# Third layer's routed experts: tiles of 128 rows in place of 256, result buffers in the room of the residual sums

## The reference

```python
def _L2_ffn_ref(x, router_w, router_bias, sw1, sw3, sw2, ew1, ew2):
    xf = x.reshape(-1, C)                                   # 2048 x 256
    shared_out = jax.nn.silu(xf @ sw1) * (xf @ sw3) @ sw2    # hidden 512
    s = jax.nn.sigmoid(xf @ router_w.T)
    _, topk_idx = jax.lax.top_k(s + router_bias, 2)          # 2 of 8 experts
    s_sel = jnp.take_along_axis(s, topk_idx, axis=1)
    denom = s_sel.sum(axis=1, keepdims=True)
    gates = jnp.where(denom > 1e-09, s_sel / (denom + 1e-09), 1.0 / 2)
    comb = jnp.einsum('nke,nk->ne', jax.nn.one_hot(topk_idx, 8), gates)
    h = jax.nn.gelu(jnp.einsum('nd,edh->neh', xf, ew1))      # hidden 256
    y = jnp.einsum('neh,ehd->ned', h, ew2)
    return shared_out + jnp.einsum('ned,ne->nd', y, comb)
```

## Time and profile before

| What | Value |
|---|---|
| Median of 3 runs | 2845.38 us |
| The profiled execution: its time, its span | 2846.69 us, 2844.9 us |
| PE busy, share of the span | 2314.1 us, 81% |
| DVE, ACT, POOL busy | 1528.4, 934.1, 815.6 us |
| Third layer's shared unit and scatter | up to about 1813 us |
| Tile loop of the third layer | 1813.4 to about 1904.6 us |
| Bytes moved by transfers | 203.25 MB, mean 71 GB/s |

### The profile page before, as it was taken

The page is one execution under the profiler, slowest core; times in us unless marked ns, Lnnn a source line. Parts: engine busy times, 40 slices in busy tenths (PEclk is TensorE's granted clock), DMA queues, the critical chain, the costliest instruction groups (busy, mean ns, idle before and its releaser), DMA issues. The chain is left out here.

```text
span 2844.9 us, 37465 instructions
## 1 busy us (share of the span) xinstructions
PE 2314.1 (81%) x14275; PEld 1526.4 (54%) x14275; DVE 1528.4 (54%) x3005; ACT 934.1 (33%) x1469; POOL 815.6 (29%) x602
## 2 busy tenths in 40 slices
PE   6978849883995982998578876997999997768998
PEld 5755535552884871887245643773434343354554
DVE  3775763465224664000743533235999989835553
ACT  3423313320112341222223320115676674423431
POOL 1120321233002102000240104014797989602221
PEclk9989969996997786999789978998999999979999
DMA  4216010002762103553100002573010110010000
GB/s 149 68 45 227 13 60 1 1 16 101 270 220 82 36 8 142 172 195 131 49 23 1 2 1 93 169 207 111 9 51 26 35 42 19 0 48 1 8 9 15
DMA packets 103793, 203.25 MB, mean 71 GB/s; under 512 B 8832, under 2 KB 79744, under 8 KB 97728
## 3 DMA queue, kind: packets, MB, share of 16 engines
q1 hardware_dynamic: 95936, 179.88, 19.0%
q0 software_dynamic: 7680, 20.98, 2.3%
HBM read 143.02 MB, written 57.80 MB: 71 GB/s over the span
## 5 line engine op out<-in xcount | busy, mean ns | idle before, releaser
L3542 POOL TENSOR_TENSOR l_attn_ring<-l_attn_ring,l_attn_c_rows 128x1024 f32<-128x1024 f32 x128 | 301.6, 2356 | 86.2 <-DVE l_attn_ring L3431 86.2
L3431 DVE TENSOR_TENSOR_SCAN l_attn_ring<-bank,l_attn_ring 128x512 f32<-128x512 f32 x256 | 299.2, 1210 | 23.4 <-ACT bank L3317 18.9
L3161 PE MATMUL bank<-l_attn_ring,identity 128*128 128x512 f32 x512 | 253.3, 618 | 36.0 <-POOL l_attn_ring L3542 29.1
L160 PE MATMUL bank<-x_features,weights 128*128 128x512 f32 x544 | 261.3, 625 | 24.4 <-ACT x_features L3281 8.4
L3317 ACT ACTIVATE bank<-l_attn_step,l_attn_minus_exp_a_log 128x508 f32<-128x508 f32 x256 | 173.6, 685 | 162.1 <-DVE l_attn_ring L3431 161.7
L160 PEld LDWEIGHTS bank<-x_features,weights 128*128 128x128 f32 x544 | 106.1, 199 | 153.9 <-issue 130.9
L3161 PEld LDWEIGHTS bank<-l_attn_ring,identity 128*128 128x128 f32 x512 | 96.8, 196 | 152.4 <-issue 105.2
L3737 PE MATMUL bank<-l_ffn_hidden_parts,l_ffn_sign_weights 128*128 128x512 bf16 x768 | 166.4, 379 | 0.0
L454 DVE TENSOR_REDUCE negmax_slots<-bank 128x16 f32<-128x2048 f32 x48 | 109.8, 2287 | 102.9 <-PE bank L346 102.6
L3425 DVE TENSOR_TENSOR l_attn_ring<-l_attn_step_times_input,bank 128x1024 f32<-128x1024 f32 x128 | 153.5, 1199 | 3.4 <-PE bank L3147 1.6
L3737 PEld LDWEIGHTS bank<-l_ffn_hidden_parts,l_ffn_sign_weights 128*128 128x128 bf16 x768 | 75.1, 98 | 90.0
(11 more groups left out here) (652 smaller groups left out, 4519.1 us busy)
## 6 DMA issues: line engine op xcount, KB each, us to landing
l_attn_tile_weights<-l_ffn_experts SPq DMA_DIRECT2D x15, 2180.0 KB, 8.9
ffn_experts_tile_weights<-l_ffn_experts_experts SPq DMA_DIRECT2D x23, 1024.0 KB, 7.6
expert_slots<-zeros SPq DMA_DIRECT2D x8, 2048.0 KB, 13.3
l_attn_c_rows<-state_outputs SPq DMA_DIRECT2D x64, 256.0 KB, 3.2
l_ffn_tile_weights<-l_ffn_experts SPq DMA_DIRECT2D x23, 512.0 KB, 4.6
expert_slots<-zeros SPq DMA_DIRECT2D x1, 5888.0 KB, 28.3
l_ffn_experts_tile_x<-expert_slots SPq DMA_DIRECT2D x23, 256.0 KB, 5.1
expert_slots<-l_ffn_experts_tile_y SPq DMA_DIRECT2D x23, 256.0 KB, 5.6
```

The source lines that it names most:

```text
L160: mm = pe.matmul(out, w[:, f, m * P:(m + 1) * P], src[:, f, :], start=start and f == 0, stop=stop and f == k - 1)
L3161: mm = pe.matmul(net.banks[SUMS[j]][:], net.ident[:], ring[n % 4][:, j, :], start=s == 0, stop=s == STATES - 1)
L3431: nc.vector.tensor_tensor_scan(ring[n % 4][:, j, :], net.banks[DECAY[j]][:], ring[n % 4][:, j, :], 0.0, ALU.mult, ALU.add).then_inc(state_ ...
L3542: tt(ring[n % 4][:], ring[n % 4][:], c_row[:, n % STATES, :].unsqueeze(1).broadcast_to([P, 2, T]), ALU.mult).then_inc(out_ready, 1)
```

## The change

The tile size becomes a number for each sublayer. It stays 256 in the first two expert sublayers and becomes 128 in the third, whose tile count goes from 23 to 4096 / 128 + 7 = 39. A tile's rows, turned rows, hidden values and result halve; its weights do not. The results go to four buffers in place of two, and these are the four blocks of `net.r`, the residual sums, which nothing else uses in this sublayer. The helper tables of `table_dve` (`past`) move for all three sublayers into the end of a context buffer. No waits are added: PE's, ACT's and DVE's loops keep their order, with half the columns in all but the second matmul, and SP's keeps its rows.

```diff
-TILE = 256
...
+TILE_ROWS = {"l0_ffn_experts": 256, "l1_ffn": 256, "l2_ffn": 128}
...
+def tile_count(name, top_k):
+
+    return ROWS * top_k // TILE_ROWS[name] + EXPERTS - 1
...
-        self.past = [sb(f"past{i}", [P, self.tiles, EXPERTS], BF16) for i in range(2)]
+        table_room = net.ctx_room[1][:].rearrange("p b d -> p (b d)")[:, NB * D - 320:].bitcast(BF16)
+        self.past = [table_room[:, i * 320:i * 320 + self.tiles * EXPERTS].rearrange("p (t e) -> p t e", t=self.tiles)
+                     for i in range(2)]
...
-        self.xt = [sb(f"tile_x{i}", [P, 2, D]) for i in range(self.x_rooms)]
+        self.xt = [sb(f"tile_x{i}", [P, self.blocks, D]) for i in range(self.x_rooms)]
...
-        self.y = [sb(f"tile_y{i}", [P, 2, D]) for i in range(2)]
+        self.y = [net.r[:, i:i + 1, :] if self.blocks == 1 else sb(f"tile_y{i}", [P, self.blocks, D])
+                  for i in range(self.y_rooms)]
...
-        return self.net.slots_dram[bass.ds(row, TILE), :].rearrange("(j p) d -> p j d", p=P)
+        return self.net.slots_dram[bass.ds(row, self.tile), :].rearrange("(j p) d -> p j d", p=P)
...
-            sp.dma_start(self.tile_rows(row[t]), self.y[t % 2][:]).then_inc(self.stored[t % 2], 16)
+            sp.dma_start(self.tile_rows(row[t]), self.y[t % self.y_rooms] if self.blocks == 1 else self.y[t % self.y_rooms][:]).then_inc(
+                self.stored[t % self.y_rooms], 16)
...
-                for j in range(2):
-                    at = f * TILE + j * P
+                for j in range(self.blocks):
+                    at = f * self.tile + j * P
...
-                mm = project(pe, net.banks[self.HIDDEN[unit % len(self.HIDDEN)]][:, (m % 2) * TILE:(m % 2 + 1) * TILE],
+                mm = project(pe, net.banks[self.HIDDEN[unit % len(self.HIDDEN)]][:, i * self.tile:(i + 1) * self.tile],
                              self.w1(t), self.xT[t % 2], m)
...
-            for j in range(2):
+            for j in range(self.blocks):
                 mm = project_tokens(pe, net.banks[self.OUT[t % 2]][:, j * D:(j + 1) * D], self.hidden[t % 2], j,
                                     self.w2(t))
...
-            if t >= 2:
-                dve.wait_ge(self.stored[t % 2], 16 * (t // 2))
-            bank = net.banks[self.OUT[t % 2]].rearrange("p (j d) -> p j d", j=2)
+            y = self.y[t % self.y_rooms]
+            y = y if self.blocks == 1 else y[:]
+            if t >= self.y_rooms:
+                dve.wait_ge(self.stored[t % self.y_rooms], 16 * (t // self.y_rooms))
+            bank = net.banks[self.OUT[t % 2]][:, 0:self.blocks * D].rearrange("p (j d) -> p j d", j=self.blocks)
...
-        experts = Sparse(net, sub, "l2_ffn", net.signals(20), route, 2, ACT.Gelu, rooms=4)
+        experts = Sparse(net, sub, "l2_ffn", net.signals(18) + net.signals(29)[24:], route, 2, ACT.Gelu, rooms=4)
```

## The result

The changed kernel takes 2864.17 us (2862.53 to 2866.48, 4 runs), the kernel before 2845.96 us (2844.79 to 2847.3, 4 runs) beside it: a ratio of 1.0064 [1.0047, 1.0082], slower by 18.2 us. Forecast were 2858.7 us (+13.3), with a range of 2850 to 2873. The profiled executions take 2863.27 and 2846.69 us, with spans of 2861.5 and 2844.9: 16.6 us apart.

The account below looks back on a forecast made before the run. PE bounds the tile loop before; after, SP's round of 2.71 us would. With 34 rounds (92.1 us), landing and last tile, the last copy ends at 1917.9 against 1904.55: +13.3 us on 2845.4, 2858.7 us, range 2850 to 2873.

Parts of the forecast that it names:

- SP's round: Third layer's tile loop: SP's instructions for one tile take 2.71 us and set the pace, for 39 rounds against 23.
- PE at 1.95: Third layer's tile loop: transposes 0.22, first matmul 0.87 and second 0.86 make 1.95 us of PE a tile.
- SP's wait on PE gone: Third layer's tile loop: SP's wait for PE, 1.14 us a tile before, disappears; PE waits for weights instead.
- records 0.109 us apart: First matmul of a tile: its eight records of 128 columns start 0.109 us apart, as the transposes do.
- landing time: Rival, chance 0.17: weights landing late through four buffers set the loop's round; 2870 us at 6.2 us, 2888 at 7.6.
- PE as bound: Rival, chance 0.05: SP has more slack than seen, so PE sets a round of 1.95 us in the loop; 2833 us.
- a cheaper issue: Rival, chance 0.10: SP's issue follows a transfer's bytes or rows, the loop's round is 2.36 us; 2847 us.
- the clock as the bound: Rival, chance 0.10: PE's idling in each tile drops its clock to 1.2 GHz in half of the rounds; 2879 us.
- The four result buffers: Third layer's results: four buffers in place of two take no wait away, since DVE only waits for PE; nothing.
- The tile table's four operations: DVE's table operations grow from 184 to 312 elements: some 0.5 us more, covered by PE's work, else 0.3 us.
- the 4.6 us here: Landing time of a tile's 512 KB of weights, taken from a profile row over the skill's 3.2 us.
- the transfers' 2.48 us a tile: Third layer's tile loop: 512 KB of weights 1.33 us plus 256 KB of rows 1.15, just below SP's round.

Follow-up runs that it names:

- e1: Changed kernel plus a second, unused read of the weight address in each of SP's rounds, third layer only: 2878.39 us, 1.0124 of the kernel before.
- e4: Kernel before (256-row tiles) plus the same unused read of the weight address in each of SP's rounds: 2843.2 us, 0.9996 of the kernel before.
- e2: Changed kernel with 256 KB of weights loaded a tile in place of 512 in the third layer: 2858.48 us, 1.0043 of the kernel before.
- e5: Changed kernel with two result buffers in place of four: 2864.07 us, 1.0066 of the kernel before.
- e9: Changed kernel without range checks on SP's address reads, and with eight weight and row buffers in place of four: 2838.86 us, 0.9973 of the kernel before.
- e3: Changed kernel without range checks on SP's two address reads a round, in all three expert sublayers: 2855.02 us, 1.0035 of the kernel before.
- e6: Changed kernel with the third layer's stores issued by ACT, with its own address load, in place of SP: 2860.11 us, 1.0055 of the kernel before.
- e8: Changed kernel's 128-row tiles with all eight experts' weights loaded once and copied on-chip by ACT and POOL: 2833.78 us, 0.996 of the kernel before.

## Why the prediction came out as it did

**Right:** the bound that replaces PE. SP's round was forecast at 2.71 us, with PE at 1.95, transfers below, SP's wait on PE gone, records 0.109 us apart, and a loop that is longer by 34 rounds and not by bytes or columns. e1, e4 and e2 show it from three sides. The rivals fell: landing time (median 4.9 us, where 5.3 decides; e2 takes it to 3.1 and leaves the usual round at 2.65), although it had its part in one round of the 34, behind the landing of 6.2 us, with SP waiting on PE as the prediction said it would show; PE as bound (16.3 us of 78 idle), a cheaper issue (0.33 to 0.38 us, whatever the bytes), and the clock as the bound (0.98 in the stretch, one dip). The four result buffers cost and bring nothing, as said, though because DVE has time to spare and not because no wait would be there (e5). The tile table's four operations grew from 0.35 to 0.48 us each, 0.5 us in all as forecast, beside PE's 13.92 us block, which had 13.90.

**The term that was mis-sized** is SP's round. Its usual size was 0.06 us shorter than forecast (2.65; the issue is a little cheaper, 0.33 for the weights and the row load), but the mean is 2.823: 34 x (2.823 - 2.71) = 3.8 us. I had read the round from two steps of an undisturbed stretch; a list that sets the pace also pays for each of its disturbances, of which the 1.14 us of slack in each round before had let none through. In the kernel before SP is late in the same way: a row load at 1862.04 is issued in 0.63 us in place of 0.37, and from the store at 1884.23 to the row load it takes 1.49 us in place of 1.16, each 0.7 or 1.1 us after such a packet of 16 KB starts. Yet all rounds there last 3.87 to 3.92 us. In the changed kernel these are the late instructions with the short waits around them (4.1 us) and one late landing with the dip of the clock behind it (1.8 us); the shorter usual round takes 2.0 of it back. The rest is small: the load of tile 4 goes out 4.88 us after the loop's start where 4.60 was forecast (0.3), landing and last tile take 8.02 us in place of 7.8 (0.2; copies of 0.42 and not 0.36, landing 4.7). Together 4.4 us: the loop is longer by 17.7 where 13.3 were forecast. Slips in the working are too small to matter: at the weight load's price a round is 2.68 and not 2.67 us, the landing time that decides is 5.3 and not 5.4, and PE's forecast share is 0.72 and not 0.75. The section of the Trainium skill that the prediction set aside (DMA: Bandwidth & Descriptors, Anatomy of one DMA) gives its sum for transfers issued by GpSimd, and these are SP's, so the 4.6 us here is no test of it.

**Wrong without consequence** was the transfers' 2.48 us a tile, from two equations with shares of two different loops. As a price it did not enter the sum. As a bound it was refuted by e9's 2.2 us at a share of 1.01. A share of 0.93 at 281 GB/s was therefore no sign of a limit: e9 moved a quarter more bytes a second at a share of 1.01.

**The clock** behaved as the row of 7.60 in 10 us let one expect: with PE idle for some 0.7 us in each round the granted clock stayed at 1.00 outside the one dip. The rule of the Trainium skill (TensorE: Matmul & The Clock Gate, A second HAM failure mode) would have had it go back and forth; the trace shows a single dip, behind the longest idle piece, 1.98 us. The length of that piece alone does not explain it: one of 1.97 us, ahead of the first matmul at 1912.72, brought no dip, and in e1, whose PE was busy for only 45.45 of 67 us (1822 to 1889) at 1.00, the one dip came behind a piece of 1.15. What calls for the dip is open.

**Open:** what holds SP up every eight to ten rounds. In its favour as a fetch of instructions: the packets and the groups of long rounds coincide four times in this loop, they persist with half of the transfers (e2, where the packets of 16 KB at 1833.75, 1861.19, 1880.76 and 1905.96 stand in its four longest rounds), and in e1, with more instructions a round, the groups begin five to eight rounds apart in place of eight to ten. Against it: the two late steps that end before their packet starts. Nothing that was run removes the fetch by itself.

## What to carry to other kernels

Halving a tile halves the matmul's columns but not the list of the engine that issues its transfers: before a tile is made smaller, count that list per tile (here 2.65 us, two address loads with range checks and three issues) and compare it with the new tile's time on PE. Slack in a profile, here 1.14 us of wait in each round, is what also swallows irregular delays; once it is gone, add them to the sum. When relief for the bound brings less than it should, look for the loop behind it (a wait that returns, as in e3 and e6), and relieve both before judging the idea: e9 and e8 turn 0.6% slower into 0.3 and 0.4% faster.

## What the runs showed of the hardware

- A load of an address into a register of SyncE with its range check costs 0.55 to 0.58 us there (e1, e4), and the check is about half: taking out two saves 0.53 us a round (e3).
- The issue of a transfer with a register address mostly took 0.33 to 0.40 us on SyncE, for 128, 256 or 512 KB alike (the changed kernel, e2).
- 355 GB/s at a share of 1.01 (e9), where 256 GB/s at 0.90 had looked near full.
- The 16 engines land 128 KB in 1.8 to 2.0 us with light traffic (e8, a share of 0.43) and in 3.9 to 4.8 us at a share of 0.92.
- Float32 matmul records of 128 columns start 0.11 us apart, though each has a weight load whose own record lasts 0.190 us.
- With PE idle for 0.7 us of 2.65 in each round the granted clock stayed at 1.00 but for one dip.
- A copy of 128x512 float32 within the on-chip memory from an address in a register takes 0.62 us on ScalarE and 0.61 on GpSimd.
